# Head projections as 64-row products into a bank each, with TensorE's row loop in two bodies

## The reference

```
q, k, v = heads of layernorm(x) @ Wq, Wk, Wv              # 4096 x 2 x 64
scores  = where(adj > 0, q k^T / 8, -9e15)                 # 2 x 4096 x 4096
sat     = softmax(scores) @ v                              # 4096 x 128, head 0 then head 1
out     = (sat[:2048] @ weightr | sat[2048:] @ weightd) + bias
x       = x + leaky_relu(out, 0.01)
h       = gelu(layernorm(x) @ W1[e] + b1[e]);  y_e = h @ W2[e] + b2[e]
x       = x + sum of y_e over the two experts with the largest gate scores
```

## Time and profile before

| | |
|---|---|
| median of 3 runs | 805.73 us (805.17 to 806.05) |
| the profiled execution | 805.47 us, of which the span of the trace is 803.7 us |
| PE busy | 775.5 us, 96% of the span |
| VectorE, ScalarE, GpSimd busy | 82%, 85%, 85% |
| TensorE's mean granted clock | 0.999 of full speed |
| chain that ended last | PE 85%, POOL 5%, DVE 4%, issue 3% |

### The profile page before, as it was taken

One profiled execution on the slowest core, in us unless ns is written; L12 is line 12 of the kernel. 1 busy time (PEld: TensorE's weight loads), 2 busy tenths in 40 slices (PEclk: granted clock), 3 DMA queues, 4 the chain that ended last, 5 costly groups with the idle time before them and its releaser, 6 DMA issues.

```text
span 803.7 us, 34483 instructions
## 1 busy us (share of the span) xinstructions
PE 775.5 (96%) x13088; PEld 577.2 (72%) x13088; DVE 658.4 (82%) x1470; ACT 684.6 (85%) x1099; POOL 681.6 (85%) x673
## 2 busy tenths in 40 slices
PE   4999999999999999999999999999999999999997
PEld 2467777777777777777777777777777677777775
DVE  6887997989989898999989899998985777545554
ACT  4678887888888888888888888888988999999996
POOL 4799998999999999999998999999986767667664
PEclk9999999999999999999999999999999999999999
DMA  8633543453335334343444335334300000000000
GB/s 230 119 61 61 83 68 62 66 84 59 61 60 81 62 62 67 59 80 59 64 72 66 62 62 85 59 59 62 55 1 2 2 15 15 15 14 13 13 13 13
DMA packets 40912, 45.11 MB, mean 56 GB/s; under 512 B 22169, under 2 KB 32161, under 8 KB 40865
## 3 DMA queue, kind: packets, MB, share of 16 engines
q0 software_dynamic: 9216, 33.56, 26.4%
q1 hardware_dynamic: 31216, 10.71, 5.7%
q10 hardware_dynamic: 432, 0.20, 0.1%
HBM read 71.72 MB, written 2.10 MB: 92 GB/s over the span
## 4 chain that ended last, share of the span: by engine, by line
PE 85%; POOL 5%; DVE 4%; issue 3%; ACT 1%; DMA 1%; DVEq 0%; POOLq 0%
PE ps L1069 19%; PE ps L1090 18%; PE ps L1123 14%; PE ps L1116 9%; PE ps L1250 4%; PE ps L1251 3%; PE ps L1252 3%; PE ps L1191 3%; PE ps L1192 3%; PE ps L1193 3%; PE ps L1134 2%; POOL w_pair L366 1%; DVE pt_raw L756 1%; POOL pt_half L350 1%; PE ps L1142 1%
## 5 line engine op out<-in xcount | busy, mean ns | idle before, releaser
L734 DVE CUSTOM_DVE_ANT_0 prob<-ps,mask 128x1024 f32<-128x1024 f32 x256 | 311.1, 1221 | 28.6 <-PE ps L1069 25.0
L350 POOL TENSOR_TENSOR pt_half<-pt_raw,pt_half 128x512 f16<-128x512 f32 x252 | 301.0, 1215 | 10.5
L533 ACT ACTIVATE prob<-prob,nmax 128x1024 f32<-128x1024 f32 x256 | 292.9, 1144 | 0.2 <-DVE nmax L742 0.2
L1090 PEld LDWEIGHTS ps<-ident,prob 64*128 64x128 f32 x4096 | 154.6, 138 | 64.2 <-issue 60.2
L1069 PE MATMUL ps<-k_half,q_row 64*128 64x512 f16 x1536 | 188.1, 376 | 1.2 <-DVE k_half L684 0.8
L1090 PE MATMUL ps<-ident,prob 64*128 64x64 f32 x4096 | 180.8, 227 | 6.6 <-DVE pt_raw L756 2.2
L460 POOL TENSOR_TENSOR prob<-prob 128x512 f16<-128x512 f32 x104 | 123.7, 1194 | 56.8 <-ACT prob L611 53.9
L346 POOL TENSOR_SCALAR pt_half<-pt_raw 128x1024 f16<-128x1024 f32 x126 | 139.1, 1104 | 24.5 <-ACT pt_raw L553 9.6
L1123 PE MATMUL ps<-pt,v_sb 128*64 128x128 f32 x2048 | 126.2, 276 | 1.5 <-issue 1.5
L962 DVE SCALAR_TENSOR_TENSOR x_sb<-ps,k_half,x_sb 128x128 f32<-128x128 f32 (+1 forms) x256 | 72.1, 344 | 64.1 <-PE ps L1252 61.4
L1069 PEld LDWEIGHTS ps<-k_half,q_row 64*128 64x128 f16 x1536 | 73.7, 95 | 61.0 <-issue 6.6
(11 more groups left out here) (124 smaller groups left out, 1122.9 us busy)
## 6 DMA issues: line engine op xcount, KB each, us to landing
mask<-in_adj POOLq DMA_DIRECT2D x64, 512.0 KB, 5.4
q_row<-q_nat SPq DMA_DIRECT2D x128, 32.0 KB, 1.9
x_sb<-in_x SPq DMA_DIRECT2D x4, 512.0 KB, 7.2
out<-x_sb SPq DMA_DIRECT2D x8, 256.0 KB, 2.3
x2t_hi<-in_L_ffn_W SPq DMA_DIRECT2D x1, 1024.0 KB, 6.3
wq_sb<-in_L_gnn_Wq ACTq DMA_DIRECT2D x1, 64.0 KB, 3.2
wk_sb<-in_L_gnn_Wk ACTq DMA_DIRECT2D x1, 64.0 KB, 4.7
wv_sb<-in_L_gnn_Wv ACTq DMA_DIRECT2D x1, 64.0 KB, 6.0
```

The lines of the kernel that those rows point to most:

```text
L350: ins = pool.tensor_tensor(pt_lo[:, q, part, :], pt_raw[:, q % 2, part, :], pt_hi[:, q, part, :], ALU.subtract)
L533: act.activation(prob[:, h, cols], prob[:, h, cols], ACT.Exp, bias=nmax[:, h:h + 1], scale=-1.0, accum_out=sums[:, j, h, p:p + 1]).then_in ...
L734: dve.tensor_tensor_reduce(out=prob[:, h, col_of(p)], in0=ps[:, 2 * (u % 2):2 * (u % 2) + 2, :].rearrange("p b c -> p (b c)"), in1=mask[:, ...
L1090: ins = pe.transpose(ps[:, bank + half, t * DH:(t + 1) * DH], prob[part, h, (p * KT + t) * P:(p * KT + t + 1) * P], ident[part, part])
```

## The change

Three things change.

1. `out_project` makes four products of 64 rows (a head's half of `sat_st` and the unpadded half of the weights) and 128 columns in place of two products of 128 rows and 256 columns. Head 0's go to bank 7 (columns 0 to 255), head 1's to columns 128 to 383 of bank 6, beside the sum of `attend`. It stands between the transposes of unit 4 and the scores of unit 4, thus ahead of `attend(i - 1, 0)`, which now waits until VectorE has read bank 6.
2. `divide` is two functions. `divide_second` reads head 1's products and stands in unit 4 of the odd row, behind VectorE's copy of unit 4; `divide_first` stays where `divide` was. They exchange heads, so that each still adds to the other. `keep_logits` moves from unit 4 to unit 3.
3. TensorE's loop over rows 6 to 31 (13 passes) becomes a loop over rows 4 to 17 and one over rows 18 to 31 (7 passes each), with the choice between the two weight matrices fixed in each. Rows 4 and 5 are no longer written out ahead.

For the last pair, in the expert stage, the products go to banks 5 and 4.

```diff
+        def o_part(banks, t, h):
+            first = h * P + t * D
+            return ps[:, banks[h], first:first + D]
...
-            def divide(t0, bank=POST):
+            def divide_second(t0, banks=(POST, AV)):
                 link = linker(post_chain, POST_STEPS // PAIR * t0 + 2)
                 dve.wait_ge(o_psum, t0 + PAIR)
                 for t in range(PAIR):
-                    ins = dve.scalar_tensor_tensor(o_half[:, t, :], ps[:, bank, t * HEADS * D:t * HEADS * D + D],
-                                                   rinv[:, t, 0:1], bias_b[:, :], ALU.mult, ALU.add)
+                    ins = dve.scalar_tensor_tensor(o_half[:, t, :], o_part(banks, t, 1), rinv[:, t, 1:2], bias_b[:, :],
+                                                   ALU.mult, ALU.add)
                 link(ins)
+            def divide_first(t0, banks=(POST, AV)):
+                link = linker(post_chain, POST_STEPS // PAIR * t0 + 3)
                 for t in range(PAIR):
-                    second = t * HEADS * D + D
-                    ins = dve.scalar_tensor_tensor(o_pre[:, t, :], ps[:, bank, second:second + D], rinv[:, t, 1:2],
-                                                   o_half[:, t, :], ALU.mult, ALU.add)
+                    ins = dve.scalar_tensor_tensor(o_pre[:, t, :], o_part(banks, t, 0), rinv[:, t, 0:1], o_half[:, t, :],
+                                                   ALU.mult, ALU.add)
                 link(ins)
...
                         copy_pt(i - 1, u, early, last)
+                    if post and par == 1 and u == 4:
+                        divide_second(i - 3)
                     if now:
                         mask_scores(i, par, u, prior)
...
-                        if u == 4 and ready:
+                        if u == 3 and ready:
                             keep_logits(i - 5)
                         if u == 5:
-                            divide(i - 3)
+                            divide_first(i - 3)
...
-            divide(NT - PAIR, bank=PREP0 + 1)
+            divide_second(NT - PAIR, banks=(PREP0 + 1, PREP0))
+            divide_first(NT - PAIR, banks=(PREP0 + 1, PREP0))
...
-            def out_project(t0, bank=POST):
+            def out_project(t0, m, banks=(POST, AV)):
                 pe.wait_ge(sat_ready, t0 + PAIR)
                 if not isinstance(t0, int) or t0 > 0:
                     pe.wait_ge(logit_ready, t0)
+                pe.nop(nofuse=True)
                 for t in range(PAIR):
-                    ins = pe.matmul(ps[:, bank, t * HEADS * D:(t + 1) * HEADS * D], sat_st[:, t, :],
-                                    wrd[:, t0 // (NT // 2), :, :].rearrange("p h d -> p (h d)"), start=True, stop=True)
+                    for h in range(HEADS):
+                        dims = slice(h * DH, (h + 1) * DH)
+                        ins = pe.matmul(o_part(banks, t, h), sat_st[dims, t, :], wrd[dims, m, h, :], start=True, stop=True)
                 ins.then_inc(o_psum, PAIR)
...
                     if prior:
                         transposes(i - 1, 2 * k, early, not now)
+                    if post and par == 1 and k == AV_BLOCK:
+                        out_project(i - 3, m)
                     if now:
                         scores(i, par, 2 * k)
...
+                    if post and par == 1 and k == AV_BLOCK:
+                        pe.wait_ge(post_chain, POST_STEPS // PAIR * (i - 3) + 3)
                     if k >= AV_BLOCK and prior:
                         attend(i - 1, k - AV_BLOCK, early)
...
-                    if post and par == 1 and k == 2:
-                        out_project(i - 3)
...
-            step(4, 0)
-            step(5, 1)
-            pairs(pe, 6, NT, step)
+            pairs(pe, 4, NT // 2 + PAIR, step)
+            pairs(pe, NT // 2 + PAIR, NT, lambda i, par: step(i, par, m=1))
```

More of the change, by code:

```diff
@@ L1154, in logits, with step @@
                 ins.then_inc(logit_psum, PAIR)
-            def step(i, par, prior=True, now=True, drain=True, post=True, ready=True, early=False):
+            def step(i, par, prior=True, now=True, drain=True, post=True, ready=True, early=False, m=0):
                 for k in range(NU // 2):
@@ L1282, in ffn @@
                     if early and e == 1:
-                        out_project(NT - PAIR, bank=PREP0 + 1)
+                        out_project(NT - PAIR, 1, banks=(PREP0 + 1, PREP0))
                     if early and e == 5:
```

## The result

The changed kernel takes 807.9 us (median of 6 runs, 807.56 to 809.67) against 805.23 (6 runs, 804.24 to 806.05) for the kernel before on the same chips: a ratio of 1.0036, 95% interval 1.0026 to 1.0046. The forecast was 803.7 with a range to 807.8 and faster as the likeliest; the kernel is slower, and the time is 0.1 us outside the range. The profiled execution took 807.89 us, its span is 806.2.

What follows compares the result with a forecast made beforehand. PE was taken to bound the kernel. Fourteen odd rows at -1.06 + 0.43 + 0.49 = -0.14 give -1.96; row 3 -0.35, expert stage -0.25, loops +0.5: -2.06, so 803.7 us, range 801.5 to 807.8.

Steps and rivals of the forecast that it cites:

- Bound by PE: Whole kernel: PE is busy 96% of the span, so a microsecond spared there comes off the end unless it returns as wait.
- Hidden, with 0.1 left: Even row: unit 7's VectorE copy ends near 315.85, TensorE needs it at 315.95, so unit 6's mask 0.4 late costs nothing.
- The stall of 0.49: Odd row, ahead of the new products: TensorE waits for VectorE's sat_ready, 0.48 to 0.50 us per pair.
- The products at 0.43: Odd row on TensorE: the four new float32 products, eight records, take 0.43 us, between bounds of 0.28 and 0.87.
- the halves do overlap: New products: forecast assumed row halves work side by side; rival without overlap: 0.87 us a group, 810.7 us, chance 0.14.
- The turning point: New products' group on TensorE: above 0.57 us each pair of rows becomes slower.
- The meeting of the mask with GpSimd: Odd row: make_mask L691, moved to about 311.75, meets GpSimd's L346 and ends 0.55 to 0.7 us behind it.
- hidden, by a tenth: Odd row, VectorE: divide_second ends at 309.14, unit 4's mask can start at 309.2, so the division costs nothing.
- VectorE's old waits of 0.69 and 0.23: VectorE: these existing waits were to absorb the lateness of its later masks and copies.
- The loops: TensorE's two loops: twelve jumps back stay twelve; first reading code in rows 18 and 19 costs +0.5 us, bounds 0 and 3.
- row 5's 1.5: TensorE's instruction wait in row 5, forecast to stay; a rival (more is gained, chance 0.13) had it fall away: -1.5 us.
- the gain is eaten: Rival: longer stall, late unit 7 copy or second body's full 1.5 us; about 805 to 806.1 us, chance 0.28.

Runs made afterwards that it cites:

- products_between: The changed kernel with the projections' products between the scores of units 4 and 5: 810.15 us, ratio 1.0054 to the kernel before.
- all_three: The changed kernel with products between the scores, divide_first ahead of make_mask and VectorE's loop cut behind unit 1 of the odd row: 804.52 us, ratio 0.9985.
- division_first: The changed kernel with divide_first ahead of make_mask in unit 5 of the odd row: 806.44 us, ratio 1.0008 to the kernel before.
- jump_moved: The changed kernel with VectorE's loop cut behind unit 1 of the odd row: 802.97 us, ratio 0.9975 to the kernel before.
- masks_early: The changed kernel with the second half of the next row's mask made in unit 1 of odd rows: 925.89 us, ratio 1.149.
- loops_only: The kernel before with only TensorE's loop in two bodies, products and division as before: 806.14 us, ratio 1.0009.

## Why the prediction was wrong

- *Bound by PE.* Right by busy time, wrong where it mattered. The step that failed is "Hidden, with 0.1 left". It followed VectorE's lateness (unit 6's mask 0.27 behind its old time; measured 0.28 relative to unit 4's transposes) to one waiter, the even row's first transposes, which indeed don't wait. The next waiter, the transposes of unit 1 on the copy of unit 0, was not asked. Between the two stood an idle of 0.47 that was listed as a wait for PE; it was VectorE's jump, and no slack. So 0.28 us of the lateness came through in each pair, where the prediction had none.
- *The stall of 0.49:* right (0.47), and so was its cause, `sat_st`.
- *The products at 0.43:* the halves do overlap. Without a wait in front the group takes 0.44 to 0.45 (`products_between`, `all_three`), as forecast; behind the wait it takes 307.79 - 307.27 = 0.52. So the term that was too small is the start behind a wait. The turning point named was 0.57; with 0.04 each for the longer groups ahead of `attend` and of the jump the sum on PE is -1.06 + 0.47 + 0.52 + 0.08 = +0.01, no gain at all in place of -0.14. The longer group ahead of `attend` isn't owed to the wait added there: in `products_between`, with the same wait, it takes 0.58 as before.
- *The meeting of the mask with GpSimd:* forecast and found (1.34 instead of 0.73; 1.6 was counted), at nearly the time given. It is the largest part of the lateness, though `division_first` doesn't part it from the second link.
- *The links* (an operation that waits until the division's results are written). Each half of the division now has its own end to wait for before a mask: idle of 0.32 and 0.23 us at VectorE, where there was one of 0.23. The first makes unit 4's mask start 308.95 - 307.79 = 1.16 behind its scores, where 0.97 was counted as before: "hidden, by a tenth" was wrong by 0.19. The second, 0.23, was left out: the prediction let "VectorE's old waits of 0.69 and 0.23" pay for the lateness, but the 0.23 stayed. It was the link before as well, though listed as a wait for PE: unit 6's mask started 313.73 - 312.68 = 1.05 behind its scores, and 0.96 in `division_first`, where it does wait for PE.
- *Luck in it.* That the lateness of unit 6's mask was forecast as 0.27 and measured as 0.28 is luck: the meeting was counted 0.3 too long, and the links were short by 0.4.
- *The loops:* +0.5 forecast, +0.5 found around row 19. The other kernels with two bodies have 0 (`division_first`) to 0.74 (`products_between`) at that place. That row 5's 1.5 might fall away was named as a rival; it did in this profile.
- *Which case came:* "the gain is eaten", by the margin on VectorE, at nearly three times its price of 0.1: 0.28 per pair on top of a gain of nothing. In the ledger of the spans that is 10 x 0.29 and 0.33, 0.46 and 0.49 in three more pairs, 4.2 in all; +0.5 for the second body, -1.6 with row 5's wait and -0.5 from the start lead to the +2.5 measured. For TensorE a jump costs 0.11 and the second body 0.5; VectorE's jump leaves it idle for 0.48, of which 0.44 go with the jump. The Trainium skill's rule on taken branches ("Runtime: NRT & Kernel Launch", "Instruction fetch mechanics") speaks of a transfer of instructions that a jump can force; VectorE's gap isn't that, since the trace of before has no transfer of instructions at all from 174.2 to 600.9 us, and the gap in every pair of the loop.

What stays open: the wait for instructions in row 5. It was 1.5 before, absent after and in `jump_moved`, 2.6 in `division_first`, whose list on TensorE is the changed kernel's. So it isn't set by the code alone. The traces show one difference. The 16 KB transfer of instructions that follows the one at 117 to 119 us starts at 123.5 us after and at 124.0 in `jump_moved`; in the seven others (`masks_early`, whose times differ, left aside) it starts at 128.0 to 129.4, and all seven have the wait (0.97 to 2.85). What delays the transfer is open. The wait also costs more than its length where it is long. In the four traces with 2.08 or more (`loops_only`, `products_between`, `all_three`, `division_first`) TensorE's mean granted clock is 0.50 to 0.67 between 132 and 136 us, behind the wait (0.50 is the lower of its two levels, 1.2 GHz), where it is 1.00 in the three with 0.97 to 1.52 (in `loops_only` the 32 records of L1123 behind the wait take 3.63 us in place of 1.97), and the pair from row 5 to row 7 takes 39.47 to 40.86 us, against 35.37 and 35.61 in the two traces without the wait. So two single runs can differ by 5 us from this place alone; the argument above rests on the periods, which lie behind it.

## What to carry to other kernels

Where an engine has become late, follow it to every instruction that waits for it, not only to the next one, and treat an idle stretch in front of a loop's first instruction as the jump, whatever releaser is named: if its length stays the same when the releaser moves, it is no slack. A loop's jump cost nothing here once the body was cut where the engine waits anyway; that one edit is worth 2.2 us in the kernel before and 4.9 in the changed one. And an operation that is put ahead of others on a nearly full engine also moves them in time against a third engine, here into a meeting that costs 0.6 us.

## What the runs showed of the hardware

A float32 product of 64 rows and 128 columns, two row halves in turn into two banks, takes 0.056 us a record (8 in 0.45), or 0.065 behind a wait (8 in 0.52), against 0.059 for two column halves (L1123: 32 in 1.90, with two changes of tile in it) and 0.217 for a full one of 256 columns.

VectorE's operation on the mask (128x2048 bfloat16 values) takes 0.69 us when it begins just ahead of GpSimd's (at 320.10 in the changed kernel, against 320.21); GpSimd's L351 then takes 1.49 in place of 1.04. When GpSimd's is under way, the mask's ends 0.55 us behind GpSimd's end, whenever it began: in the changed kernel (311.44 + 1.34 against 311.20 + 1.03), in `jump_moved` (1.27 long), in `products_between` (1.17) and in `division_first` (0.71). In the even row it takes 1.77 though it begins 0.17 ahead of L346; there GpSimd's issue of a transfer (0.60 from 328.34) is under way at its start. So what the meeting costs is what is left of GpSimd's operation when the mask's begins. That one of the two is held for the other is argued from these ends; no run takes GpSimd's operation away.
